# Near bias as a factor on VectorE instead of an addition on TensorE, in a two-layer cross-attention kernel

## The reference, cut to what matters

```python
# layer 0
q, k = _rope(q, cos[:L_q], sin[:L_q]), _rope(k, cos[:L_kv], sin[:L_kv])
scores = jnp.einsum('bhqd,bhkd->bhqk', q, k) * SCALE
scores = scores + _temporal_bias(L_q, L_kv)[None, None, :, :]
attn = jax.nn.softmax(scores, axis=-1)
attended = jnp.einsum('bhqk,bhkd->bhqd', attn, v)
...
# layer 1: the same attention with its own weights and a mask, without a bias
...
out = jnp.einsum('bsef,bse->bsf', y, comb) / K     # 8 experts, 2 chosen per token
```

## Time and profile before

| | us |
|---|---|
| median of three runs | 569.89 |
| the profiled execution, its own time | 571.24 |
| span in its profile, first to last instruction | 567.8 |
| PE busy (share) | 505.2 (89%) |
| ACT busy | 433.0 (76%) |
| DVE busy | 280.4 (49%) |
| POOL busy | 171.2 (30%) |
| matmuls of the near bias, L519, 416 of them | 42.2 busy, 200 ns each |
| exponentials, L1173, 416 of them | 1.025 each |
| GpSimd's five additions and subtractions on a 128x496 chunk, L1015 to L1023 | 0.97 to 1.17 each |

### The profile page before, as it was taken

One profiled execution on the slowest core, in us unless ns is written; L12 is line 12 of the kernel. 1 busy time (PEld: TensorE's weight loads), 2 busy tenths in 40 slices (PEclk: granted clock), 3 DMA queues, 4 the chain that ended last, 5 costly groups with the idle time before them and its releaser, 6 DMA issues.

```text
span 567.8 us, 15324 instructions
## 1 busy us (share of the span) xinstructions
PE 505.2 (89%) x6318; PEld 256.2 (45%) x6318; DVE 280.4 (49%) x741; ACT 433.0 (76%) x493; POOL 171.2 (30%) x207
## 2 busy tenths in 40 slices
PE   7677798899889998999999999899989999998994
PEld 4344454445444554455555444444444444343332
DVE  4853665774586455654523252325434543261156
ACT  1235587677768787687898999899988998899841
POOL 4464945486488124871001000100000000000003
PEclk9897999999999999999999999999999999999998
DMA  8575884579557802575184356229411840000000
GB/s 264 157 231 161 258 289 112 158 223 306 142 161 214 304 16 75 166 218 163 27 178 141 110 123 158 60 46 202 119 55 47 178 145 2 12 1 1 8 6 15
DMA packets 51583, 74.52 MB, mean 131 GB/s; under 512 B 11146, under 2 KB 40050, under 8 KB 51506
## 3 DMA queue, kind: packets, MB, share of 16 engines
q1 hardware_dynamic: 40258, 37.54, 26.4%
q0 software_dynamic: 5632, 24.07, 12.9%
q10 hardware_dynamic: 5616, 11.86, 6.7%
HBM read 39.95 MB, written 18.83 MB: 104 GB/s over the span
## 4 chain that ended last, share of the span: by engine, by line
PE 60%; ACT 15%; issue 10%; DVE 8%; POOL 4%; DMA 2%; ACTq 0%; DVEq 0%; POOLq 0%
PE ps L538 26%; PE ps L514 16%; ACT probs L1173 9%; PE ps L449 4%; PE ps L439 2%; PE ps L668 2%; ACT ctx_turned L1173 2%; DVE k_swapped L1473 1%; PE ps L443 1%; ACT ctx_tokens L1173 1%; DMA k_scratch<-k_parts 1%; ACT k_parts L1198 1%; PE ps L702 1%; PE ps L550 1%; PE ps L519 1%
## 5 line engine op out<-in xcount | busy, mean ns | idle before, releaser
L1173 ACT ACTIVATE probs<-ps 124x1024 f32<-124x1024 f32 (+1 forms) x305 | 296.2, 1025 | 56.1 <-PE ps L519 44.6
L514 PE MATMUL ps<-q_side,k_side 64*124 64x256 bf16 (+1 forms) x1664 | 161.9, 290 | 38.3 <-ACT probs L1173 30.1
L538 PE MATMUL ps<-probs,values 124*9 124x256 f32 (+1 forms) x2440 | 162.8, 382 | 0.0
L514 PEld LDWEIGHTS ps<-q_side,k_side 64*124 64x124 bf16 (+1 forms) x1664 | 79.4, 130 | 144.9 <-ACT probs L1173 77.4
L538 PEld LDWEIGHTS ps<-probs,values 124*9 124x9 f32 (+1 forms) x2440 | 52.7, 90 | 63.5 <-issue 16.7
L1043 POOL TENSOR_TENSOR post_rstd<-post_rstd,power 128x2 f32<-128x2 f32 x12 | 8.4, 703 | 194.2 <-DVE post_rstd L1688 126.7
L519 PE MATMUL ps<-bias_near,bias_w 64*124 64x84 bf16 (+1 forms) x416 | 42.2, 200 | 0.0
L1173 ACT ACTIVATE ctx_tokens<-ps 124x1024 f32<-124x1024 f32 (+1 forms) x37 | 38.0, 1026 | 4.9 <-PE ps L514 4.0
L1473 DVE SCALAR_TENSOR_TENSOR k_swapped<-ps,beta_products,k_table_sb 32x496 f32<-32x496 f32 (+2 forms) x64 | 40.4, 632 | 0.9
L1173 ACT ACTIVATE ctx_turned<-ps 124x1024 f32<-124x1024 f32 (+1 forms) x37 | 37.9, 1025 | 3.4 <-PE ps L514 2.4
L1173 ACT ACTIVATE ctx_normed<-ps 124x1024 f32<-124x1024 f32 (+1 forms) x37 | 37.9, 1025 | 2.4 <-PE ps L514 1.6
(11 more groups left out here) (250 smaller groups left out, 634.7 us busy)
## 6 DMA issues: line engine op xcount, KB each, us to landing
k_side<-k_scratch SPq DMA_DIRECT2D x24, 400.2 KB, 7.8
k_scratch<-k_parts POOLq DMA_DIRECT2D x16, 372.0 KB, 4.9
k_side<-k_parts SPq DMA_DIRECT2D x45, 124.0 KB, 2.4
q_side<-q_parts SPq DMA_DIRECT2D x63, 64.0 KB, 2.5
v_scratch<-values POOLq DMA_DIRECT2D x4, 936.0 KB, 9.9
values<-v_scratch SPq DMA_DIRECT2D x4, 936.0 KB, 14.3
v_scratch<-v POOLq DMA_DIRECT2D x12, 288.0 KB, 4.7
mask_q<-in_mask POOLq DMA_DIRECT2D x8, 400.5 KB, 4.2
```

The lines of the kernel that those rows point to most:

```text
L514: last = pe.matmul(ps[0:width, bank, SQ * i:SQ * (i + 1)], kst[rows, j % 2, 2 * g + i, at], qst[rows, query_slot(j, run), 2 * g + i, :], s ...
L538: last = pe.matmul(ps[32 * i:32 * i + VC, ACC + g // 2, SQ * (g % 2):SQ * (g % 2) + SQ], v[0:rows, j % 2, t, h, :], probs_of(u)[0:rows, SQ ...
L1173: act.activation(probs_of(u)[0:rows, :], ps[0:rows, s:s + 2, :].rearrange("p a n -> p (a n)"), ACT.Exp)\
```

## The change

1. The two matmuls per unit at L519 are gone, and with them the table `bias_w` in the main path. A table `near_factor`, the exponential of the near bias in float32, is loaded in place of `near_q`. After ACT's exponential, VectorE multiplies the 42 near queries of four heads by it, in place (`weigh_near`, 124 x 4 x 42 elements, 208 instructions). The `values` matmuls of items 0 to 3 wait for that multiply.
2. VectorE's order names at each of its waits up to which unit it has multiplied by then (`near_by`), and once in the middle of `rotate_keys`.
3. In items 0 to 2 PE takes the values one or two units later: 1 (item 0) or 0 units in the first pair, 2 in each pair, 3 or 4 in the last, and before the side work instead of between. `probs` gets a fifth slot from item 1 on (8 from item 3).
4. GpSimd's first chunk store goes ahead of a memset and of the wait for `scores_ready`.
5. At the end ACT copies one half of the last sums and one half of `y`; `token_norm` goes ahead of two checks; the second half's eight scaled outputs are summed by PE with an identity matrix, together with `x` and the expert bias, and ACT copies the sum out. GpSimd's `add_last` is gone.

```diff
 def values_at(j, pair):
     if j < WIDE_FROM:
-        return 2
+        last = 2 * NG * KT // 4 - 1
+        return (1 if j == 0 else 0) if pair == 0 else (3 if j == 0 else 4) if pair == last else 2
...
-            return u % 4 if u < WIDE_FROM * UB else (u - WIDE_FROM * UB) % 7
+            return u % 4 if u < UB else (u - UB) % 5 if u < WIDE_FROM * UB else (u - WIDE_FROM * UB) % 8
...
             def scores(u):
...
-                if bias:
-                    for half, bank in enumerate(banks):
-                        rows = slice(HALF * half, HALF * half + HALF)
-                        last = pe.matmul(ps[0:width, bank, :].rearrange("p (i n) -> p i n", n=SQ)[:, :, first_near(run):first_near(run) + NEAR],
-                                         G["bias_w"][rows, at], near[rows, t:t + 1, :].broadcast_to((HALF, 2, NEAR)),
-                                         start=False, stop=True, skip_group_check=True)
...
             def values(u):
-                pe.wait_ge(probs_ready, u + 1)
+                if j < NB:
+                    pe.wait_ge(near_weighed, u + 1)
+                else:
+                    pe.wait_ge(probs_ready, u + 1)
...
                 for w in (u + 2, u + 3):
                     if w < NJ * UB:
                         scores(w)
-                beside(j, 2 * pair)
+                if j >= WIDE_FROM:
+                    beside(j, 2 * pair)
                 for i in range(values_at(j, pair)):
                     values(taken)
                     taken += 1
+                if j < WIDE_FROM:
+                    beside(j, 2 * pair)
                 beside(j, 2 * pair + 1)
...
             for k in (2, 3):
                 experts(NB - 1, k)
+            pe.matmul(ps[:, ACC, 0:D], comb_t[:, 128 * (TT - 1):128 * TT], eb[:], start=False, stop=False, skip_group_check=True)
+            for i, e in enumerate(SCALED_LAST):
+                pe.wait_ge(last_scaled, i + 1)
+                last = pe.matmul(ps[:, ACC, 0:D], ident[:], p[:, 0, D * e:D * e + D], start=False, stop=i == E - 1, skip_group_check=True)
...
+            store_keys(0, 0)
             ones_of_values(1)
             pool.wait_ge(scores_ready, 5)
-            for n in range(2):
-                store_keys(0, n)
+            store_keys(0, 1)
...
+            def weigh_near(j, i):
+                nonlocal weighed
+                while weighed < UB * j + i:
+                    b, t, g = weighed // UB, weighed % UB // NG, weighed % NG
+                    n0, rows = first_near(t // 2), rows_of(t)
...
+                    at = probs_of(weighed)[0:rows, :].rearrange("p (h n) -> p h n", n=SQ)[:, :, n0:n0 + NEAR]
+                    dve.wait_ge(probs_ready, weighed + 1)
+                    dve.tensor_tensor(at, at, near[0:rows, t:t + 1, :].broadcast_to((rows, HG, NEAR)), ALU.mult).then_inc(near_weighed, 1)
+                    weighed += 1
+
+            def near_by(j, slot):
+                weigh_near(j, min(2 * (slot // 2) + 2, UB))
...
-            def rotate_keys(b, n):
+            def rotate_keys(b, n, j=0, slot=-2):
+                near_by(j, slot)
...
                 for to in range(0, 128, 32):
+                    if to == 64 and slot >= 0:
+                        weigh_near(j, min(2 * (slot // 2) + 3, UB))
...
             project(NB - 1)
+            token_norm(NB - 1)
             check_finite(NJ - 1)
             least_of_checks()
-            token_norm(NB - 1)
```

More of the change, by code:

```diff
@@ L160 @@
 CENTRE_EXPERTS_AT = ((NB, 42), (NB, 46))
+SCALED_LAST = (0, 1, 4, 5, 2, 3, 6, 7)
 def expert_at(j, slot):
@@ L490, in scores @@
                 j, t, g = u // UB, u % UB // NG, u % NG
-                bias, n = j < NB, [t0 for t0, _ in CHUNKS].index(t) if t in [t0 for t0, _ in CHUNKS] else None
+                far, n = j < NB, [t0 for t0, _ in CHUNKS].index(t) if t in [t0 for t0, _ in CHUNKS] else None
                 width = rows_of(t)
@@ L1557, in copy_sums @@
                     dve.wait_ge(made[HIGH], side.of(HIGH, "pick", j - 1))
-                for n in range(2):
+                if j < NB:
+                    weigh_near(j, UB)
+                for n in range(2 if j < NJ - 1 else 1):
                     dve.wait_ge(probs_used, UB * (j + 1) - 2 + 2 * n)
```

210 lines of the change are left out of this document (134 added, 76 removed).

## The result

The changed kernel takes **617.66 us**, median of four runs (611.69 to 618.13), against 570.45 us for the kernel before, run beside it (567.97 to 572.94). The ratio is 1.080, 95% interval 1.075 to 1.085: 8% slower. The forecast was 564 us with a range up to 574. The profiled execution took 617.97 us, span 616.3, mean granted clock of PE 0.942 (before 0.984). In all that follows medians are of every execution, ratios leave out the two that were over 1.5% above the fastest of their kernel (611.9 us of c1, 621.7 us of g2), and g2's profile is of that slower one.

The account below looks back on a forecast made before the run. PE was taken to bound items 0 to 2, ACT items 3 to 7, one chain the end. Terms: -6.4 - 5 + 7 - 1.7 = -6.1 us; against the 569.89 us median, forecast 564 us, range 554 to 574.

Parts of the forecast that it names:

- near matmuls: PE, items 0 to 2: removing four near matmuls saves 0.10 us per pair over 64 pairs, 6.4 us gained.
- early store: Start of item 0: GpSimd's first store goes out sooner, ACT resumes about 4.4 us earlier; 5 us gained.
- moved side work, late values: PE's order, items 0 to 2: moving side work costs nothing; later values give the multiply 1 to 2 us of cover.
- multiply: VectorE, between exponential and values: 0.333 us each plus holds by GpSimd, hidden except where VectorE is full; 7 us lost.
- end: Last sums after ACT's last scaling: identity matmul and ACT copy replace GpSimd's last addition; 1.7 us gained.
- The sign to watch: Near 40 us in item 0: no idle ACT, with item 0 about 5 us shorter, would show the forecast right.
- Moving side work behind the values changes no sum on PE: nothing.: PE's list in items 0 to 2: side work issued after the values was costed at zero.
- that wait should be over by then, and I cost it at nothing beyond the multiply itself: VectorE's list: each multiply's wait for its exponential, with PE's emptied side banks behind it, costed at nothing extra.
- the three stretches where VectorE is fullest: Parts of items 0 to 2, one at 154.0 to 176.5: multiplies add 3.6, 2.8 and 1.9 us, taken as 7.
- the slow case: Items 0 to 2: long holds by GpSimd make VectorE set the pace; 586 us (576 to 590), chance 14%.
- VectorE becomes the bound: Rival, items 0 to 2: holds of 0.82 us per multiply make VectorE need 22.7 us over their length; 586 us, 14%.
- nothing, at most 1 us: Item 3, pairs taking all existing values: they wait about 0.33 us more, with two exponentials queued on ACT.

Follow-up runs that it names:

- c1: Changed kernel with the even slot's side work back between scores and values in items 0 to 2, multiply kept: 601.4 us, ratio 1.050.
- g2: Changed kernel with VectorE's second look at the mask in item 3 moved behind the multiplies: 614.6 us, ratio 1.074.
- b1: Kernel before with its near matmuls taken out (near bias left out), nothing else changed: 567.4 us, ratio 0.9945.
- d1: Kernel before with only GpSimd's first chunk store moved ahead of its memset and wait: 566.5 us, ratio 0.9948.
- a1: Changed kernel without VectorE's multiply, near bias left out, values waiting for the exponential alone: 579.2 us, ratio 1.015.
- c3: Changed kernel without the multiply, with ACT's copy of the second keys one slot later: 564.6 us, ratio 0.989.
- c4: Whole changed kernel, multiply included, with ACT's copy of the second keys one slot later: 603.1 us, ratio 1.061.
- c2: Changed kernel without the multiply, even slot's side work back before the values in items 0 to 2: 573.9 us, ratio 1.005.
- e3: Kernel before with the early store, ACT's copy of the second keys one slot later, and the changed kernel's end: 561.0 us, ratio 0.983.
- g1: Changed kernel with each multiply cut from 42 queries to one per head, all instructions and waits kept: 597.1 us, ratio 1.047.
- a2: Changed kernel with the multiply replaced by a maximum over the same elements, one input in SBUF, same waits: 594.0 us, ratio 1.041.
- a3: Changed kernel with the multiply written to a scratch tile, PE waiting for the exponential alone: 590.7 us, ratio 1.038.
- f1: Changed kernel with two matmuls of zeros before PE's wait for the multiply, every second unit of items 0 to 2: 625.6 us, ratio 1.097.
- e4: Kernel before with early store, later ACT copy and the new end, plus matmuls of zeros before the last-weights wait and each identity matmul: 564.5 us, ratio 0.986.

## Why the prediction was wrong

| term | forecast | measured | by |
|---|---|---|---|
| near matmuls | -6.4 (3 to 7.8) | -2.7 to -3.1 | b1 |
| early store | -5 (2 to 7) | -3.0 (by medians -4.6) | d1 |
| moved side work, late values | 0 | +15 | a1, c3 |
| multiply | +7 (0 to 23) | +38.5 (+27.5 in the other order) | a1, c3, c4; c1, c2 |
| end | -1.7 (1 to 2.5) | 0 (-1.0 at full clock) | e3; c4 |
| sum | -6.1 | +47 to +48 | |

- **The near matmuls.** Of the 0.10 us per pair of the earlier trace rows only some is on the path: items 0 to 2 of b1 change by -1.2, +0.8 and -1.0 us. Item 3, where I had put the gain at nothing because ACT sets the pace, is 1.0 us shorter (54.7 to 53.7), of which item 4 gives back 0.5.
- **The early store.** The mechanism held: ACT restarted 4.7 us earlier (forecast 4.4). The sign to watch, no idle ACT near 40 us, did not come: 3.44 us stayed, 3.96 in the changed kernel, and the end moved by 3.0 us. I had looked only at the store, not at how long its landing takes.
- **"Moving side work behind the values changes no sum on PE: nothing."** The first step that failed. The sum on PE is indeed unchanged; what changed is when ACT's input is ready, and ACT's list has its copy at a fixed place. I had listed VectorE, PE and slots as who waits, and never asked where ACT's own list reads what the moved matmul writes. The price is 15 us. One number in ACT's list gives 15 back, but 5 of them it gives in the old order too, so some 5 to 6 us remain. Taking the values later, which I counted as cover alone, has its share: in c2 it holds ACT's slots for 25.7 us.
- **The multiply.** The instruction was sized well (329 ns for 333), and so was the held time as a whole (29.3 us for 30). The step that failed is "that wait should be over by then, and I cost it at nothing beyond the multiply itself", together with the way the term was summed: extra VectorE time in the three stretches where VectorE is fullest, everywhere else hidden. No engine was full over an item, and it cost 38.5 us. The loop goes from exponential to multiply to values to PE's next scores to exponential, one or two units deep. PE takes its list in order, so each late multiply stops the scores too. The cover did not hold: without holds 23.6 us come back, about as much as was held, and PE's 21 waits for a multiply (23.1 us) are for late ones, by a hold (10.5 us) or mostly by what stood ahead in VectorE's list (12.7 us). How the rest of the 38.5 us splits between the two and the clock is not shown.
- **The signs** that I gave for the slow case were a mean above 0.6 us and VectorE over 90% busy. Both stayed low (0.48 us, 72% in item 1) and the kernel was slower than that case. The rival "VectorE becomes the bound" had the right sign for a wrong reason, capacity; its 586 us had nothing for list waits.
- **Item 3**, "nothing, at most 1 us": 4.0 us. For 3.3 of them it was not the multiply's length in pairs that take all values, which was the case I had named, but the mask's transfer ahead of it in VectorE's list (g2).
- **The end.** "An identity matmul and a copy, some 0.3 us each": the matmuls in 16 passes ended 2.8 us after the scaling, and the copy 3.1 us, where 0.8 was forecast. GpSimd's additions, which they replace, had ended 2.66 us after it. The mis-sized term is the passes and the clock they run at: 1.79 us in c4 at full clock. In c4, without the fall, the end was shorter by the forecast's lower bound.

What stays open is the clock's share: g1, a2 and a3 each raise the clock and shorten the items, but f1 raised the clock and did not, with the fillers' own price in it. Of the five terms two failed, by 15 and 31.5 us; the other three were within 3.7 us.

## What to carry over

A step that puts one engine between two others in a loop a few units deep is not hidden because that engine has free time. List every instruction and wait that stands ahead of it on its engine, and what may hold it, and compare the delays, the longest first, with the depth; a cautious first price for the holds is their whole sum (29.3 us here, of which 23.6 came back without them). When a matmul is moved in PE's order, look up each reader's own list for the place where it reads, and move that too; here one slot was worth 15 us in the new order and 5 in the old. Before a large change is given up or kept, run its parts alone, and in both orders where order is part of it: a small part and one number together gain 1.4% here without the rest.

## What the runs showed of the hardware

- A VectorE instruction with two inputs in SBUF can be held by several GpSimd instructions in a row, by the profile also by ones that start after it (56.20 to 59.36 us above; 3.95 us at the longest). All 17 multiplies over 1 us ended 0.18 to 0.20 us behind a GpSimd instruction. One of four elements per partition is held nearly as long (3.36 us) as one of 168.
- With one input in SBUF, same elements and place, none of 208 took over 0.33 us, and the kernel was 23.6 us faster.
- PE's granted clock fell to 0.50 during or behind pauses of 1 to 3.4 us and stayed there 3 to 10 us; in the changed kernel this makes some 52 us in items 0 and 1. Where it fell in e4, PE had been busy 1.69 of the last 2.80 us.
- Eight f32 identity matmuls of 128x128 run as 16 passes and took 2.05 us at full clock (c4), 3.78 at half (e3), and 3.40 where the clock fell during them.
